# Expert weights fetched a stage earlier, other orders at two stage entries, one-hot tiles on GpSimd too, and TensorE warmed at two entries

## The reference

```
x = x + L0_attn(norm(x))     # gated recurrence, attention over a window of 32
x = x + L0_ffn(norm(x))      # attention over the batch, then a mixture of experts
x = x + L1_attn(norm(x))     # retention, 16 heads
x = x + L1_ffn(norm(x))      # silu(x @ gate.T) * (x @ up.T) @ down.T, 768 hidden

# the mixture of experts in L0_ffn: 4096 tokens, 8 experts, the best 2 of each token
top_p, top_i = top_k(softmax(x @ router), 2);  top_p /= sum(top_p)
order = argsort(top_i.reshape(-1), stable)     # 8192 (token, expert) pairs
within = place of a pair in its expert;  kept if within < 1280
padded_tokens[expert * 1280 + within] = x[token]
out = gelu(padded_tokens @ w1[e]) @ w2[e]      # for each expert, 1280 x 256
h1 + sum over a token's slots of prob * out[slot]
```

## Time and profile before

| | |
|---|---|
| median of 3 runs | 1881.45 us (1878.49 to 1881.6) |
| the profiled execution | 1882.23 us, of which the span from first to last instruction is 1879.1 us |
| TensorE busy | 1657.3 us (88% of the span), mean granted clock 0.942 |
| VectorE, ScalarE, GpSimd busy | 1051.6 us, 606.2 us, 500.7 us |
| stages in the span | route 933 to 970.5, experts 970.8 to 1291, retention 1291 to 1607, swiglu from 1607 |

### The profile page before, as it was taken

How to read it: one execution, slowest core, us unless ns; L and a number is a source line. 1 busy time by engine, 2 the same in 40 slices (tenths; PEclk the granted TensorE clock), 3 DMA queues, 4 the chain that set the end, 5 groups by cost and what they waited for, 6 DMA issues and landing times. The chain is left out here.

```text
span 1879.1 us, 32520 instructions
## 1 busy us (share of the span) xinstructions
PE 1657.3 (88%) x10448; PEld 1275.2 (68%) x10448; DVE 1051.6 (56%) x2675; ACT 606.2 (32%) x1801; POOL 500.7 (27%) x636
## 2 busy tenths in 40 slices
PE   4999899999999692677849999998899998799998
PEld 3777677777777461567838888886666666455655
DVE  4555457777777768998541222222888887222221
ACT  1333255544555240122341111111444444111110
POOL 2222210000000117875113223232554552100000
PEclk9999899999999895777769999998999999899999
DMA  8666500000000000000233223322101100000000
GB/s 219 111 115 114 99 13 13 12 13 13 12 12 1 9 1 6 1 23 25 71 109 90 90 89 91 116 65 102 30 28 33 28 28 7 1 22 11 22 11 22
DMA packets 92256, 88.32 MB, mean 47 GB/s; under 512 B 11456, under 2 KB 82048, under 8 KB 91776
## 3 DMA queue, kind: packets, MB, share of 16 engines
q1 hardware_dynamic: 74368, 57.80, 13.0%
q0 software_dynamic: 6912, 18.88, 3.7%
q10 hardware_dynamic: 10880, 10.49, 1.6%
HBM read 46.64 MB, written 23.20 MB: 37 GB/s over the span
## 5 line engine op out<-in xcount | busy, mean ns | idle before, releaser
L794 ACT ACTIVATE probs<-psS,nm 128x256 f32<-128x256 f32 x256 | 119.2, 470 | 183.1 <-DVE nm L827 183.1
L1645 DVE COPY YE<-e_psY 128x512 f32<-128x512 f32 x40 | 27.7, 692 | 220.5 <-PE e_psY L1591 220.5
L1581 PE MATMUL e_psH<-e_XT,w 128*128 128x256 f32 x640 | 146.2, 382 | 0.0
L1591 PE MATMUL e_psY<-w,e_HT 128*128 128x256 f32 x640 | 144.0, 379 | 0.0
L1551 POOL DMA_INDIRECT XE<-token_rows,held x80 | 76.2, 952 | 228.1 <-PE e_psX L1568 179.0
L825 DVE TENSOR_REDUCE mx<-psS 128x2 f32<-128x512 f32 x128 | 87.9, 687 | 84.1 <-PE psS L715 81.9
L715 PE MATMUL psS<-Rec,QT 128*128 128x256 f32 (+1 forms) x512 | 132.3, 381 | 0.9 <-ACT QT L782 0.9
L1591 PEld LDWEIGHTS e_psY<-w,e_HT 128*128 128x128 f32 x640 | 121.6, 190 | 16.5
L1581 PEld LDWEIGHTS e_psH<-e_XT,w 128*128 128x128 f32 x640 | 119.9, 192 | 15.1
L441 PE MATMUL psKV<-wkv,XT 128*128 128x384 f32 (+1 forms) x384 | 122.2, 469 | 1.4 <-ACT XT L491 1.4
L1621 ACT ACTIVATE e_HT<-e_psH 128x512 f32<-128x512 f32 x80 | 47.8, 597 | 233.1 <-PE e_psH L1581 226.6
(11 more groups left out here) (258 smaller groups left out, 3542.4 us busy)
## 6 DMA issues: line engine op xcount, KB each, us to landing
KD<-KV SPq DMA_DIRECT2D x256, 66.0 KB, 2.5
expert_out<-YE ACTq DMA_DIRECT2D x40, 256.0 KB, 2.2
w<-in_w SPq DMA_DIRECT2D x16, 512.0 KB, 4.4
X<-in_x SPq DMA_DIRECT2D x8, 512.0 KB, 7.4
x_turned<-XT SPq DMA_DIRECT2D x32, 128.0 KB, 2.3
XS<-x_turned SPq DMA_DIRECT2D x8, 512.0 KB, 4.0
token_rows<-o_XN SPq DMA_DIRECT2D x32, 128.0 KB, 1.7
out_x<-X SPq DMA_DIRECT2D x8, 512.0 KB, 2.9
```

Source lines behind the costliest of these rows:

```text
L794: nc.scalar.activation(probs[:, b.q % 4, hg, :], psS[b.q % 2][:, hg, :], ACT.Exp, bias=nm[:, b.q % 2, hg:hg + 1], scale=scale, accum_out=s ...
L1581: mm = pe.matmul(psH[c % 2][half][:, m, :], w1[:, s, kc, f:f + P], XT[:, c % 2, kc, :], start=(m == 0 and kc == 0), stop=(m == 1 and kc == ...
L1591: mm = pe.matmul(psY[c % 2][:, j, :], HT[:, c % 2, m, j * P:(j + 1) * P], w2[:, s, m, :], start=(j == 0 and m == 0), stop=(j == 1 and m == ...
```

## The change

Four edits. The expert weights become an object that is allocated around `route`, `experts` and `retention`; SP fetches the first two experts' weights in `route`, ahead of the retention weights, and the loop in `experts` starts at 1. In `route` the last of `tile_of`'s eight parts in each group is made by GpSimd, with one instruction from float32 `iota`, and ScalarE makes three. In `experts` GpSimd clears semaphores only after the first four gathers, and TensorE starts with 24 matmuls that nobody reads. In `swiglu` TensorE starts with 14 such matmuls, ScalarE with a silu of one column, and GpSimd makes the roots before it clears.

```diff
@@ -146,8 +146,9 @@
                 position_qkv(k)
                 position_attention(k)
             w = RetentionWeights(k, c2)
-            route(k, w)
-            experts(k)
+            expert_w = ExpertWeights(k, c2)
+            route(k, w, expert_w)
+            experts(k, expert_w)
             retention(k, w)
         swiglu(k)
...
@@ -1380,6 +1381,8 @@
             sp.dma_start(before[:, :], a["before"]).then_inc(weights, 16)
             sp.dma_start(iota[:, :], a["iota"]).then_inc(weights, 16)
             sp.dma_start(token[:, :], a["token"]).then_inc(weights, 16)
+            for s in range(2):
+                next_w.load(sp, s, s)
             following.load(sp)
 
         @block.gpsimd
...
@@ -1388,6 +1391,13 @@
             pool.wait_ge(weights, 48)
             nc.gpsimd.tensor_scalar(minus[:, :], token[:, :], -1.0, None, ALU.mult).then_inc(other_set, 1)
             nc.gpsimd.tensor_copy(columns[:, :], iota[:, :]).then_inc(columns_set, 1)
+            pool.wait_ge(placed, 2)
+            for n in range(NG):
+                if n >= 2:
+                    pool.wait_ge(group_used, n - 1)
+                t = (n + 1) * (G // 2) - 1
+                nc.gpsimd.tensor_scalar(tile_of[:, n % 2, G - 1, :], iota[:, 0:NA], place[:, t, 1:2], token[:, t:t + 1],
+                                        ALU.is_equal, ALU.mult).then_inc(last_made, 1)
 
         @block.tensor
         def _(pe):
...
@@ -1404,6 +1414,7 @@
             for n in range(NG):
                 pe.wait_ge(row_made, n + 1)
                 pe.wait_ge(tile_made, n + 1)
+                pe.wait_ge(last_made, n + 1)
                 for x in range(G):
                     mm = pe.matmul(psI[n * 2 // NG][:, :], row_of[:, n % 2, x, :], tile_of[:, n % 2, x, :],
                                    start=(n % (NG // 2) == 0 and x == 0), stop=(n % (NG // 2) == NG // 2 - 1 and x == G - 1))
...
@@ -1418,12 +1429,12 @@
             for n in range(NG):
                 if n >= 2:
                     act.wait_ge(group_used, n - 1)
-                for x in range(G // 2):
+                for x in range(G // 2 - 1):
                     t = n * (G // 2) + x
                     ins = nc.scalar.activation(apart[:, n % 2, x, :], iota[:, 0:NA], ACT.Square, bias=other[:, t:t + 1])
                 ins.then_inc(apart_made, 1)
                 act.wait_ge(apart_made, n + 1)
-                for x in range(G // 2):
+                for x in range(G // 2 - 1):
                     t = n * (G // 2) + x
                     ins = nc.scalar.activation(tile_of[:, n % 2, x * 2 + 1, :], apart[:, n % 2, x, :], ACT.Relu,
                                                bias=token[:, t:t + 1], scale=minus[:, t:t + 1])
...
@@ -1502,15 +1513,30 @@
             nc.vector.tensor_scalar(k.held[:, :], late[:, 1, :], -1.0, 0.0, ALU.add, ALU.max).then_inc(held_ready, 1)
 
 
-def experts(k):
+class ExpertWeights:
+
+
+    def __init__(self, k, ctx):
+        self.w1 = k.sb(ctx, "w1", [P, 2, KC, FE])
+        self.w2 = k.sb(ctx, "w2", [P, 2, FE // P, D])
+        self.loaded = [k.sem(ctx, f"e_w_loaded{s}") for s in range(2)]
+        self.a = k.a
+
+    def load(self, sp, s, e):
+
+        for dst, src in ((self.w1, self.a["w1"]), (self.w2, self.a["w2"])):
+            sp.dma_start(dst[:, s, :, :], src[bass.ds(e, 1), :, :].rearrange("a (k p) n -> p (a k) n", p=P)
+                         ).then_inc(self.loaded[s], 16)
+
+
+def experts(k, weights):
 
     nc, a = k.nc, k.a
     CH = 2 * P
     NCH = CAP // CH
     with ExitStack() as ctx:
         k.open_stage(ctx)
-        w1 = k.sb(ctx, "w1", [P, 2, KC, FE])
-        w2 = k.sb(ctx, "w2", [P, 2, FE // P, D])
+        w1, w2, w_loaded = weights.w1, weights.w2, weights.loaded
         lnw, lnb = k.sb(ctx, "e_w", [P, KC]), k.sb(ctx, "e_b", [P, KC])
         XE = k.sb(ctx, "XE", [P, 2, 2, D])
...
@@ -1534,18 +1559,18 @@
         def _(sp):
             sp.dma_start(lnw[:, :], a["ln2w"]).then_inc(consts, 16)
             sp.dma_start(lnb[:, :], a["ln2b"]).then_inc(consts, 16)
-            with sp.Fori(0, NE // 2) as i:
+            with sp.Fori(1, NE // 2) as i:
                 for s in range(2):
 
                     sp.wait_ge(y_ready, i * N + (s + 1) * NCH)
-                    sp.dma_start(w1[:, s, :, :], a["w1"][bass.ds(i * 2 + s, 1), :, :].rearrange("a (k p) n -> p (a k) n", p=P)).then_inc(w_loaded[s], 16)
-                    sp.dma_start(w2[:, s, :, :], a["w2"][bass.ds(i * 2 + s, 1), :, :].rearrange("a (k p) n -> p (a k) n", p=P)).then_inc(w_loaded[s], 16)
+                    weights.load(sp, s, i * 2 + s)
 
         @block.gpsimd
         def _(pool):
-            k.clear_finished()
             assert NE == NB
             for g in range(NE * NCH):
+                if g == 2:
+                    k.clear_finished()
                 pool.wait_ge(x_ready, g + 1)
                 for j in range(2):
                     pool.indirect_dma_start(XE[:, g % 2, j, :], None, k.rows_dram[:, :], bass.IndirectOffsetOnAxis(
...
@@ -1559,6 +1584,8 @@
         def _(pe):
             pe.sem_inc(y_ready, N)
             pe.sem_inc(x_ready, 2)
+            for n in range(24):
+                pe.matmul(psX[:, 0, 0:P], k.ident[:, :], k.ident[:, :], start=True, stop=True)
 
             def turn(i, c):
                 pe.wait_ge(x_loaded[c % 2], i * (32 * N // 2) + 32 * (c // 2 + 1))
...
@@ -2253,6 +2280,8 @@
                         mm = pe.matmul(psY[u % 2][:, :], HT[:, m, u * P:(u + 1) * P], wd[:, m, :], start=(m == 0), stop=(m == M - 1))
                     mm.then_inc(y_ready, 1)
 
+            for n in range(14):
+                pe.matmul(psY[0][:, 0:P], k.ident[:, :], k.ident[:, :], start=True, stop=True)
             turn(0)
             with pe.Fori(1, NB) as i:
                 gate_up(i - 1)
...
@@ -2265,6 +2294,8 @@
         def _(act):
             act.sem_inc(t_evac, 2)
             act.sem_inc(g_done, 2)
+            nc.scalar.activation(SG[:, 1, 0:1], k.ident[:, 0:1], ACT.Silu).then_inc(tried, 1)
+            act.wait_ge(tried, 1)
 
             def turned(i):
                 act.wait_ge(t_ready, i + 2)
...
@@ -2331,8 +2362,8 @@
 
         @block.gpsimd
         def _(pool):
+            rows.roots(pool)
             k.clear_finished()
-            rows.roots(pool)
 
 
 def lay_out(x):
```

More of the change, by code:

```diff
@@ L1326, in _, with route @@
             turns(dve, turn)
-def route(k, following):
+def route(k, following, next_w):
     nc, a = k.nc, k.a
@@ L1363, in route @@
         apart = k.sb(ctx, "apart", [P, 2, G // 2, NA])
-        columns_set = k.sem(ctx, "o_columns_set")
+        columns_set, last_made = k.sem(ctx, "o_columns_set"), k.sem(ctx, "o_last_made")
         other_set, apart_made = k.sem(ctx, "o_other_set"), k.sem(ctx, "o_apart_made")
@@ L1522, in experts @@
         consts = k.sem(ctx, "e_consts")
-        w_loaded = [k.sem(ctx, f"e_w_loaded{s}") for s in range(2)]
         x_loaded = [k.sem(ctx, f"e_x_loaded{s}") for s in range(2)]
@@ L2213, in swiglu @@
         psY = [k.ps(ctx, f"f_psY{s}", [P, D]) for s in range(2)]
-        casts = k.sem(ctx, "f_casts")
+        casts, tried = k.sem(ctx, "f_casts"), k.sem(ctx, "f_tried")
         xn_ready, t_ready, t_evac = k.sem(ctx, "f_xn_ready"), k.sem(ctx, "f_t_ready"), k.sem(ctx, "f_t_evac")
```

## The result

The changed kernel takes 1868.49 us (median of 5 runs, 1864.37 to 1869.63) against 1878.57 for the kernel before on the same chip. The ratio is 0.9938, interval 0.9928 to 0.9949: 11.6 us less (9.6 to 13.5) where 9.2 were forecast. The profiled execution was the shortest of the five (1864.37), and its span is 16.6 us shorter than that of before. So the trace holds some 5 us that aren't in the comparison of runs, and I first cut it into stages by the starts of the same instructions: SP's first transfer of route and of experts, the third transposes in experts, SP's first transfer of retention, VectorE's first statistics in swiglu, and the second gate product.

The account below looks back on a forecast made before the run. TensorE was taken as the bound in steady experts, with slack in route and at two stage entries; 2.3 + 4.8 + 2.1 = 9.2 us gave 1872.2 us against 1881.45, range 1867.5 to 1876.5.

Parts of the forecast that it names:

- Route, 2.3 forecast: Route: moving a quarter of ScalarE's tiles to GpSimd lets VectorE set the pace; gain 2.3 us, between 1.1 and 4.1.
- most of them should meet it ... I take 1.8 of the 3.0: Route: most of GpSimd's eight new instructions hold VectorE up, costing 1.8 us of a possible 3.0.
- The rival without any hold: Route: GpSimd holds nothing up, route gives 4.1 us, the sum is 11.0, the time 1870.4; chance 0.16.
- the 0.37 of the forecast: Route: assumed time in us of GpSimd's new 128 x 80 instruction, taken from a 128 x 128 cast of the same types.
- The Trainium skill: Route: its rule locks the VectorE and GpSimd port pair for whichever starts first; by it all eight instructions would count.
- Experts, 4.8 forecast: Entry of experts: early weights, gathers ahead of clears and 24 warming matmuls bring third transposes 4.8 us sooner (4.3 or 5.4).
- the third transposes come at 13.0 to 14.3 (as the prediction said): Entry of experts, a sign: third transposes 13 to 14.3 us after SP's first issue, where it was 18.5.
- 7.1 us of warming in place of 7.0: Entry of experts: 24 warming matmuls take 7.04 us as in route, or 8.2 if the clock rises late.
- the second gather 1.0 us sooner: Entry of experts: without four weight transfers and 14 clears ahead, the second gather starts at 973.1, not 974.13.
- Swiglu, 2.1 forecast: Entry of swiglu: 14 warming matmuls bring the second pair of products sooner; gain 2.1 us (1.5 or 2.7).
- The roots: Entry of swiglu: roots ahead of 42 clears make tiles up to 1.0 us earlier, worth only 0 to 0.2 us.
- ScalarE's early silu: Entry of swiglu: loading ScalarE's table early is worth nothing, as its first silu isn't needed before the third pair.

Follow-up runs that it names:

- u_scalar8: The changed kernel with ScalarE making four parts of tile_of again and GpSimd none; ratio to the kernel before 0.9964.
- w_routeonly: The kernel before with the route edit alone (GpSimd makes one part of tile_of in a group, ScalarE three); ratio 0.9971.
- v_castlate: The changed kernel with VectorE's cast of the gate weights in swiglu moved behind the first four normalised tiles; 1867.99 us in one run.
- v_pool2: The changed kernel with two of tile_of's eight parts in each group on GpSimd, three each on VectorE and ScalarE; ratio to the kernel before 0.9943.
- u_nowarm: The changed kernel without the 24 warming matmuls at the entry of experts; ratio to the kernel before 0.9931.

## Why the prediction was wrong in one step, and where it was right

**Route, 2.3 forecast, 4.2 found. This is the step that failed.** The term is "most of them should meet it ... I take 1.8 of the 3.0": 1.8 us of time in which GpSimd holds VectorE up. The runs show some 0.4 us, and that it is GpSimd that waits. Its instruction took 1.71 us in place of 0.37, VectorE's large ones kept their 1.21, and since one in a group stays inside the 2.03 us of VectorE's pace, the wait costs nothing. u_scalar8 puts the edit's worth at 4.2 us in the trace and 4.9 in the runs, and w_routeonly finds 4.1 from `pick` to the end of the stage on the kernel before. The 1.9 us that route gave beyond its term are most of what lies between the 9.2 forecast and the 11.6 measured. The rival without any hold, 11.0 us in sum, is what came, though GpSimd's instruction took 0.63 to 0.69 us even with no large one beside it, and not the 0.37 of the forecast.

The row that I argued from was read beside the wrong instruction. None of GpSimd's 2.0 us copies at L659 lies beside a long scaling. All six long ones lie beside its next copy, which starts 0.15 us ahead of them. Here the second of the two scalings starts at 283.26 and takes 1.99:

```profile
283.11 1.99 POOL L666 COPY Rec<-window_mask 64x2048 f32 x1 [0.24 <-POOL R L659]
283.00 2.26 DVE L834 TENSOR_SCALAR probs<-probs,rs 128x256 f32<-128x256 f32 x2
```

The Trainium skill ("SBUF — State Buffer", section "SBUF: two separate sides"), as cited in the prediction, says that whoever starts first keeps the port. This pair agrees, and so does the cast at the entry of swiglu, which starts 0.17 us ahead of the root and holds it (v_castlate takes that hold away). Route does not, by the starts in the trace. Of the seven instructions beside a large one, four start 0.10 to 0.24 us ahead of it, and yet they end behind it and VectorE's keeps its length:

```profile
953.65 1.87 POOL L1399 TENSOR_SCALAR tile_of<-iota,place,token 128x80 f16<-128x80 f32 x1
953.88 1.21 DVE L1498 TENSOR_TENSOR row_of<-columns,row_in 128x1024 f16<-128x1024 f16 x1
```

In v_pool2 GpSimd started 0.16 us ahead of a large one four times. Three times it took 1.88 us and held nothing, and once it took 0.67 and the large one 1.35. So the order of these starts doesn't tell which side waits, and what does stays open.

**Experts, 4.8 forecast, 5.4 in this trace.** Over the nine traces with early weights and 24 matmuls the third transposes come at 13.0 to 14.3 (as the prediction said), 13.4 in the mean, against 18.5 and 17.8 without these edits: 3.5 to 5.5 us. The terms were right: 7.1 us of warming in place of 7.0 (8.5 in u_scalar8, where the clock rose later), 0.60 for the first transposes, the second gather 1.0 us sooner after SP's first issue (2.35 for 3.35), and the weights' transfers as what delays it (a wait of 2.9 us from the gather's start in u_nowarm, 6.5 with the transfers). No run put the 14 clears back alone. One thing was wrong: I priced the warming as part of the gain. It takes as much as it gives (13.01 without it), because 24 last longer than the gather; 12 give 1.3 us. So the 4.8 came out with the right size while one of its causes, the warming, earned none of it. The second chunk's gather, which I had not costed, then limits.

**Swiglu, 2.1 forecast, 1.7 found.** Warmed with 14: 11.2 to 11.9 in eleven traces. Not warmed: 12.89, 13.44, 13.57. The warming does it alone. The roots gave nothing that shows, as costed at 0 to 0.2, but for another reason as well, the cast. ScalarE's early silu was tried in no run of its own.

**The bounds.** The prediction's 1868.3 to 1873.8 us has a slip: 12.4 and 6.9 us below 1881.4 are 1869.0 and 1874.5. And 1868.49 stands beside a median of 1878.57 for the kernel before, 2.9 us below the 1881.45 that the forecast started from, so the times compare less well than the differences.

**Retention, nothing forecast, 3.7 found in the trace.** The clock by stretch, 15 to 24 us after SP's first issue, is before

```profile
1306.24:1309.24 3.00, 0.01 (x1) 0.01 (x1) 2.75 (x6) 0.34 (x1) 2.77 (x4) 0.83 0.30 87
1309.24:1312.24 3.00, 3.00 (x9) 2.59 (x10) 0.18 (x1) 0.99 (x3) 1.89 (x3) 0.50 0.16 40
1312.24:1315.24 3.00, 3.00 (x4) 0.67 (x2) 0.00 (x0) 1.08 (x5) 0.12 (x1) 0.53 0.17 53
```

and after

```profile
1295.18:1298.18 3.00, 0.42 (x3) 0.14 (x1) 2.57 (x5) 0.37 (x1) 2.08 (x3) 1.00 0.31 87
1298.18:1301.18 3.00, 2.51 (x11) 1.83 (x12) 0.61 (x2) 1.79 (x7) 1.89 (x4) 1.00 0.00 0
1301.18:1304.18 3.00, 1.83 (x34) 0.98 (x32) 2.20 (x5) 0.27 (x2) 1.42 (x2) 1.00 0.29 87
```

In the sixteen traces, each of a code of its own, retention is 312.6 to 316.8 us, and it follows the time at the low clock around its entry and in its first 32 us. That is some 3 us in the three traces of 312.6 to 312.8, 7 in those of 313.0 and 313.7, 10 in the seven of 314.4 to 314.7, and 14 in the four of 316.2 to 316.8. The thirteen traces with early weights span all of it; the three without have 314.5 to 316.5, inside that spread; both ends occur with 24 matmuls of warming in experts, and 312.6 without route's edit. So the changes don't decide it as far as these traces tell, and I read it as an execution's luck. The five runs of the changed kernel differ by 5.3 us, with mean clocks of 0.949 to 0.951. That is argued: no code was traced twice, and three traces can't exclude a small influence of the weights. What makes the clock fall in a run stays open: filling one pause moved the dip.

## What to carry to other kernels

Warm TensorE at a stage's entry only for as long as the data is late, and price both: what the matmuls take, and what the low clock would cost behind them. An engine with slack can take work from the one that paces, even if its instruction takes 2.5 times as long beside the other's, as long as it stays inside the period. And cut a trace into stages by the same instructions before believing its total: here 5 of 16.6 us stood in stretches whose code was not changed.

## What the runs showed of the hardware

- GpSimd's 128 x 80 compare took 0.63 to 0.69 us alone or beside VectorE's small one-hots. Beside its large one (1.21 us) it took up to 1.88 and ended 0.34 to 0.56 us behind it in 99 of 101 cases in fourteen traces, whether it started up to 0.24 us before the large one or after. Its root of four columns took 1.0 us, and 2.5 beside VectorE's cast.
- A VectorE scaling of 0.35 us took 1.99 beside a GpSimd copy of 1.99 that had started 0.15 us ahead of it, six times in the trace of before.
- An indirect gather let TensorE go on 2.9 us after it started with no weights in transfer, and 6.5 us after beside 2 MB of weights.
- The same run of 24 float32 matmuls from the low clock took 7.1 us in one execution and 8.57 in another (the 24 of route, in the changed kernel and in w_routeonly).
